# Second attention of a two-layer block: order of the rotary products, of the last stage's weight pieces, and of P times keys and projection

## What is computed

```python
def xattn(q, kv, seg_id, ...):                      # second layer, b=4, lq=256, lk=64, 16 heads
    q_c = q @ W_dq                                  # 256 -> 96
    q_rope = _rope((q_c @ W_qr).reshape(...))       # 64 rotary columns a head
    scores = (q_nope . k_nope + q_rope . k_rope) / sqrt(192)
    attn = softmax(where(in_window, scores, NEG))
    return (attn @ v).reshape(b, lq, H * HD) @ W_o
def _rope(x): x1, x2 = halves(x); return concat(x1*cos - x2*sin, x1*sin + x2*cos)
def ffn(x): return qlinear(silu(qlinear(x, gate)) * qlinear(x, up), down)    # 256 -> 704 -> 256
x = x + xattn(layernorm(x), ctx, seg_id); x = x + ffn(layernorm(x))
```

## Time and profile before

| | us |
|---|---|
| median of three runs (range) | 849.6 (848.35 to 850.79) |
| the profiled execution | 852.24 |
| its span, first to last instruction | 850.4 |
| TensorE busy | 790.1 (93%) |
| VectorE busy | 661.8 (78%) |
| ScalarE busy | 537.9 (63%) |
| GpSimd busy | 460.7 (54%) |

### The profile page before, as it was taken

The page is one execution under the profiler, slowest core; times in us unless marked ns, Lnnn a source line. Parts: engine busy times, 40 slices in busy tenths (PEclk is TensorE's granted clock), DMA queues, the critical chain, the costliest instruction groups (busy, mean ns, idle before and its releaser), DMA issues.

```text
span 850.4 us, 14334 instructions
## 1 busy us (share of the span) xinstructions
PE 790.1 (93%) x4848; PEld 676.2 (80%) x4848; DVE 661.8 (78%) x1584; ACT 537.9 (63%) x1236; POOL 460.7 (54%) x759
## 2 busy tenths in 40 slices
PE   3777999999999999999899999999999999798998
PEld 2566888888888888888788878898888877577787
DVE  7988888899888998879789794866654689966534
ACT  6888877788768886788674555433332278864332
POOL 3585869779686896858755576442210016970000
PEclk9779999999999999999999999999999999899999
DMA  7000120011200120000200324966421010100001
GB/s 239 14 1 1 38 75 1 2 39 42 72 1 1 38 79 34 2 2 2 67 25 13 126 63 102 233 172 243 131 64 49 1 44 13 50 14 0 1 1 50
DMA packets 28265, 45.59 MB, mean 54 GB/s; under 512 B 3937, under 2 KB 18081, under 8 KB 28065
## 3 DMA queue, kind: packets, MB, share of 16 engines
q1 hardware_dynamic: 26800, 41.31, 16.5%
q10 hardware_dynamic: 1392, 3.37, 1.1%
HBM read 43.49 MB, written 1.18 MB: 53 GB/s over the span
## 4 chain that ended last, share of the span: by engine, by line
PE 60%; DVE 23%; ACT 10%; issue 4%; DMA 2%; SPq 1%; ACTq 0%; POOL 0%; DVEq 0%
PE PS L770 16%; PE PS L840 7%; PE PS L725 6%; PE PS L630 5%; PE PS L699 4%; PE PS L661 4%; PE PS L951 3%; PE PS L671 2%; DVE cat L1541 2%; PE PS L652 2%; PE PS L682 2%; PE PS L709 2%; DVE st L1635 1%; DVE yb L1537 1%; DMA l_KM<-share 1%
## 5 line engine op out<-in xcount | busy, mean ns | idle before, releaser
L2222 POOL TENSOR_SCALAR raw<-raw,mvq,rsq 128x128 f32<-128x128 f32 x312 | 186.8, 612 | 7.2 <-DVE mvq L1682 5.7
L770 PE MATMUL PS<-xq,WH 128*128 128x512 f32 x472 | 148.4, 396 | 1.0 <-ACT l_x2T L995 1.0
L770 PEld LDWEIGHTS PS<-xq,WH 128*128 128x128 f32 x472 | 86.4, 190 | 18.1 <-issue 2.1
L770 PE MATMUL PS<-xq,WL 128*128 128x512 f32 x236 | 92.4, 391 | 0.0
L630 PE MATMUL PS<-WH,xq 128*128 128x256 f32 (+1 forms) x256 | 89.3, 367 | 2.6 <-issue 1.5
L630 PE MATMUL PS<-WL,xq 128*128 128x256 f32 (+1 forms) x256 | 84.6, 348 | 0.0
L1109 ACT ACTIVATE P<-PS,sm 128x256 f32<-128x256 f32 x128 | 60.6, 491 | 30.4 <-DVE sm L1710 30.3
L1635 DVE BATCH_NORM_STATS2 st<-raw 128x6 f32<-128x128 f32 x320 | 71.9, 277 | 0.9 <-ACT raw L1081 0.9
L840 PE MATMUL PS<-xq,m_hh 128*128 128x256 f32 x384 | 69.8, 282 | 2.8 <-ACT m_hh L995 1.4
L725 PE MATMUL PS<-PH,cat 128*128 128x256 f32 x256 | 66.0, 296 | 5.8 <-DVE cat L1541 5.5
L699 PE MATMUL PS<-PT,vr 128*128 128x256 f32 x256 | 66.3, 381 | 0.7 <-ACT PT L995 0.7
(11 more groups left out here) (305 smaller groups left out, 2193.8 us busy)
## 6 DMA issues: line engine op xcount, KB each, us to landing
wst<-in_wgu SPq DMA_DIRECT2D x24, 256.0 KB, 3.8
l_KM<-share SPq DMA_DIRECT2D x16, 384.0 KB, 4.2
wst<-in_wall SPq DMA_DIRECT2D x18, 256.0 KB, 3.1
l_KM<-share SPq DMA_DIRECT2D x16, 256.0 KB, 5.1
dst<-in_wdn SPq DMA_DIRECT2D x24, 128.0 KB, 3.2
wst<-in_wkvx SPq DMA_DIRECT2D x8, 256.0 KB, 3.4
l_KM<-share SPq DMA_DIRECT2D x16, 128.0 KB, 4.3
m_pre<-in_wo ACTq DMA_DIRECT2D x1, 2048.0 KB, 8.4
```

What stands on the lines that cost most here:

```text
L770: t = e.matmul(PS[:, b, :], W[wi][:, gu, k, :], a[:, k, cols], start=(n == 0), stop=(n == 5))
L2222: t = e.tensor_scalar(v, v, mvq[:, par, n, 0:1], rsq[:, par, n:n + 1], ALU.add, ALU.mult)
```

## The change

In `turn_q` the two products with the sine of a part come first, then the two products with the cosine; the sine products no longer signal, and the sums on GpSimd wait for the PSUM bank that the cosine product frees. All nine weight pieces stand behind the last sum on GpSimd. The loop over chunks has 11 steps in place of 12: `values` and `project` come one or two places sooner, and `turn_p`, `f_turn`, `f_front` stand elsewhere in a step, with matching places in the streams of ScalarE and VectorE.

```diff
-FPIECES = ((0,), (1, 2), (3, 4), (5,), (6, 7, 8))
@@ late_order
-    for n in range(12):
+    for n in range(11):
+        if n in (5, 7, 9):
+            do("turn_p", n - 2)
         if n < 8:
             do("scores", n)
-        if n % 2 == 0 and n > 3:
-            do("values", (n - 4) // 2)
-        if 1 < n < 10:
+        if n in (2, 3):
             do("turn_p", n - 2)
         for m in QUERIES.get(n, ()):
             do("queries", m // 2, m % 2)
-        if n % 2 and n > 4:
-            do("project", (n - 5) // 2)
-        if n % 2 and n > 6:
-            do("f_turn", (n - 7) // 2)
-        if n > 9:
-            do("f_front", *FFN[n - 10])
+        if n % 2 == 0 and n > 3:
+            do("project", (n - 4) // 2)
+        if n in (4, 6, 8):
+            do("turn_p", n - 2)
+        if n % 2 == 0 and n > 5:
+            do("f_turn", (n - 6) // 2)
+        if n > 8:
+            do("f_front", *FFN[n - 9])
+        if n % 2 and n > 2:
+            do("values", (n - 3) // 2)
@@ scalar
-            for n in range(12):
-                if n % 2 == 0 and n > 3:
-                    take_lv((n - 4) // 2)
-                if 1 < n < 10:
+            for n in range(11):
+                if 1 < n < 10 and n not in (4, 6, 8):
                     take_lp(n - 2)
                 for m in QUERIES.get(n, ()):
                     swap_q(m // 2, m % 2)
+                if n == 9:
+                    gate_f(0)
+                if n % 2 and n > 2:
+                    take_lv((n - 3) // 2)
                 if n < 8:
                     exps2(n)
-                if n == 11:
+                if n in (4, 6, 8):
+                    take_lp(n - 2)
+                if n == 10:
                     split_g(0)
-                if n % 2 and n > 6:
-                    split_f((n - 7) // 2)
-                if n > 9:
-                    gate_f(n - 10)
+                if n % 2 == 0 and n > 5:
+                    split_f((n - 6) // 2)
+                if n == 10:
+                    gate_f(1)
@@ vector, turn_q
                 for u in range(2 * part, 2 * part + 2):
+                    s = tqs[4 * bb + u].rearrange("p (a t) -> p a t", a=2)
+                    w.wait_ge(swapped.sem, swapped.at[bb, u])
+                    t = e.tensor_tensor(s, s, sin, ALU.mult)
+                t.then_inc(dv.sem, 1)
+                dv.up()
+                for u in range(2 * part, 2 * part + 2):
                     n = 4 * bb + u
-                    two = [v.rearrange("p (a t) -> p a t", a=2) for v in (tqc[n], tqs[n])]
-                    b = w.filled(("qr", bb, u))
-                    q = PS[:, b, :].rearrange("p (a t) -> p a t", a=2)
                     if n > 3:
                         w.wait_ge(added.sem, added.at[units_q[n - 2 if n > 5 else n - 4]])
-                    w.wait_ge(swapped.sem, swapped.at[bb, u])
-                    e.tensor_tensor(two[0], q, cos, ALU.mult).then_inc(free[b], 1)
-                    e.tensor_tensor(two[1], two[1], sin, ALU.mult).then_inc(turned_q.sem, 1)
+                    b = w.filled(("qr", bb, u))
+                    e.tensor_tensor(tqc[n].rearrange("p (a t) -> p a t", a=2), PS[:, b, :].rearrange("p (a t) -> p a t", a=2),
+                                    cos, ALU.mult).then_inc(free[b], 1)
@@ vector, the loop
-            for n in range(12):
+            for n in range(11):
...
-                if n in (6, 8, 10):
-                    add_l((n - 6) // 2)
-                if n == 11:
+                if n in (5, 7, 9):
+                    add_l((n - 5) // 2)
+                if n == 10:
                     split_g(0)
-                if n % 2 and n > 6:
-                    split_f((n - 7) // 2)
-                if n == 11:
+                if n % 2 == 0 and n > 5:
+                    split_f((n - 6) // 2)
+                if n == 10:
                     add_l(3)
-                if n > 9:
-                    gate_f(n - 10)
+                if n > 8:
+                    gate_f(n - 9)
@@ gpsimd
-                    w.wait_ge(turned_q.sem, turned_q.at[bb, u])
+                    w.emptied(("qr", bb, u))
...
-                for j in FPIECES[n]:
-                    load_f(j)
+            for j in range(9):
+                load_f(j)
```

More of the change, by code:

```diff
@@ L513, in program @@
         swapped = count("swapped", [(bb, u) for bb in range(4) for u in range(4)])
-        turned_q = count("turned_q", [(bb, u) for bb in range(4) for u in range(4)])
         gated_5 = count("gated_5", range(2))
```

## The result

The changed kernel takes 870.2 us (median of four runs, 864.54 to 872.31) against 849.93 before: ratio 1.023, 95% interval 1.0179 to 1.0281. The direction was forecast, the size was not: 861.6 was predicted, with a range of 849 to 868. The latter has a span of 867.7 us, 17.3 more than the 850.4 before. `f_front(2,0)`, behind which both kernels do the same work, starts at 820.12 us against 802.90: all of the difference, 17.2 us, lies ahead of it.

The account below looks back on a forecast made before the run. It took TensorE's gaps to stand behind VectorE, which GpSimd holds up. X at 776.7 plus 37.8 us put f_front(2,0) at 814.5 against 802.90: +11.6, with a slow project(3) +12, on 849.6 gives 861.6; range 849 to 868.

Parts of the forecast that it names:

- TensorE up to the first f_turn: TensorE from 701.3: 55.4 us of work plus 5.6 of short gaps, reaching f_turn(0) at 762.6, 3.9 us of work ahead.
- Laying out from X on: Both engines from turn_p(5) to the start of f_front(2,0): 37.8 us, so 814.5 against 802.90 before.
- X: Time when turn_p(5) may start on TensorE, after add_l(0), soft(6) and scale(5) on VectorE: 776.7 us.
- add_l(0) beside the pieces: First feed-forward normalisation on VectorE: fourteen small instructions each held by a GpSimd one, 15.8 us in place of 4.8, +11.
- The products of turn_q: VectorE, queries: sine products no longer held by GpSimd sums, with missing weight pieces sparing about 4 us over the stretch.
- The weight pieces' own time and the sums: GpSimd: sums end at about 745.5, then 28 us of pieces run to 773 at the earliest.
- Not held: Rival: GpSimd pieces hardly hold the normalisation; -2 us, 847.5; chance 0.09 for 846 to 850.
- gaps closed: Rival: TensorE's earlier project and values fill three gaps, nothing held; about -6, 843.5; chance 0.09 for 840 to 846.
- the rival that had both normalisations held: Late pieces make add_l(1) on VectorE pay as well as add_l(0): +17, 866.6; chance 0.06 for 866 to 870.

Follow-up runs that it names:

- Experiment 2: Changed kernel with project(0) moved behind turn_p(2), turn_p(3) and scores(5), nothing else: 859.7 us, ratio 1.0101.
- Experiment 3: Changed kernel with project's output and f_turn's transposes in bank 7 for batches 0 and 2, bank 6 for 1 and 3: 865.0 us, ratio 1.0183.
- Experiment 1: Changed kernel with the nine weight pieces between the sums on GpSimd again, order and sine products as changed: 864.8 us, ratio 1.0171.
- experiment 11: Kernel before with all weight pieces behind the sums and nothing else: 856.7 us, ratio 1.0082.
- experiment 4: Kernel before with sine products first and all weight pieces behind the sums, old TensorE order and 12 steps kept: 854.4 us, ratio 1.0058.
- experiment 5: Kernel before with the sine products first alone, pieces between the sums and order as before: 852.1 us, ratio 1.0035.
- the mended order: Changed kernel with project(0) behind scores(5), project's output banks by turns, and pieces 3 to 8 only after the first normalisation: 852.9 us, ratio 1.0045.

## Why the prediction was wrong

**TensorE up to the first f_turn: this step failed.** The prediction listed gaps of 5.6 us, "none of the length that slowed TensorE before", and had project(0) start as soon as the queries ended. It counted the queries' waits for their own banks, but not the bank of project. Bank 7 carried queries (3,3), whose cosine product stands behind scale(3) on VectorE; the prediction itself put that product at 743.5 (measured 742.1), and never asked what else wanted the bank. The wait that it put at nothing was 6.05 us, and project(0) ran 2.6 us slow behind it. TensorE stood at `f_turn(0)` at 770.5 and not at 762.6 (the list itself sums to 762.3). Experiment 2 shows what this wait costs: without it the kernel is 10.5 us faster.

**Laying out from X on: the same omission.** 37.8 us were given, 820.12 - 777.05 = 43.1 were measured, so this term was 5.3 us short. project(2) was given 1.3 us of copies and 6.9 of work; it waited 3.5 us for bank 7 and took 10.08, 5.4 us more, which is the difference. Experiment 3 took 5.2 us back by a bank number.

**add_l(0) beside the pieces: right in kind, mis-sized.** 15.8 us were predicted from 754.55 on, 10.0 us measured from 761.73 on. Two errors are in it. It began 7.2 us later, for the first omission. And the sum counted one GpSimd instruction for each of fourteen small ones; in the trace six of the twelve smallest pass unheld. Experiment 1 prices the hold at 5.4 us net, experiment 11 the moved pieces at 7.8 on the old order. X came out as 776.7 against 777.05 measured by luck: a missing 7.2 us against an excess of 5.8 in the chain and of 1.0 behind it, where scale(5) was to be held once more and the pieces were over.

**The products of turn_q: right over its stretch, no gain at the end.** About 4 us were given for the new form together with the missing pieces. In experiment 4, which has both, project(0) starts 41.5 us behind the first scores, before 45.4 (746.63 less 701.28): 3.8 us. Neither does it alone: 46.2 with the sine products first (experiment 5), 44.9 with the pieces away (experiment 11). Waits further on take the gain back: alone the new form is a loss of 0.35%.

**The weight pieces' own time and the sums** were right: the sums ended at 744.1 (745.5 predicted), the pieces at 773.0 (773).

**The rivals.** "Not held" and "gaps closed" are excluded by the trace. The time is just above the rival that had both normalisations held (866 to 870), for another reason: `add_l(1)` met no pieces and took 4.8 us. The forecast of a loss was right, but it was argued from a hold that lengthened the chain by 5.2 us and not by 11, while two bank waits that cost some 14 us by their rows (6.05 + 2.6, and 3.5 + 3.0 less 1.3 for copies) were missing. The losses taken out one at a time sum to 10.5 + 5.4 + 5.2 = 21.1 us by the medians, all together to 17.3; by the stage of the profiled executions it is 7.4 + 3.6 + 3.5 = 14.5 against 17.9. So the three account for most of the loss, but whether they overlap is not shown. What stays open is why the mended order is still 0.45% slower than before; its waits for copies fit the size, and so does the 0.35% of the sine products first, and no run took either away.

## What to carry to other kernels

When a producer is moved ahead in an order that also deals out PSUM banks, write down for each moved fill who held the bank last and where that release stands on its engine; here the release, not the data, cost most. A block of GpSimd work that is moved belongs beside VectorE work like soft, whose scalings out of PSUM (L2085) took 1.27 us for two beside L2353 and 1.28 without it, not beside a chain of small two-tensor instructions. And a wait taken away on TensorE pays only up to the next one: look at what the engine then meets, as soft(7) behind `add_l(0)` here.

## What the runs showed of the hardware

A small VectorE instruction that is held goes through with the end of GpSimd's instruction, and the one behind it passes unheld when GpSimd leaves a gap of 0.08 to 0.09 us: L1607 ended at 765.61, L1611 ran from 765.64 to 765.80, and L2349 of GpSimd, 0.09 us behind its predecessor's end, started at 765.69. Where GpSimd's instructions follow without such a gap (L2353 ends 765.02, L2345 starts 764.99) the next small one was held. In this chain all five such gaps between 763.6 and 769.7 let one through, and both places without a gap held. GpSimd leaves the gap where its next instruction waits for the one before; that this is the reason is argued from the kernel, no run changed it. So seven small ones went beside four GpSimd instructions (764.99 to 769.02), and the chain took 10.0 us in place of the 15.8 predicted. The hold goes both ways: L2349 of GpSimd, 1.27 us elsewhere, took 2.37 from 760.59 on, beside the product of scale(4) (L2101, 760.59 to 761.82). The Trainium skill, GPSIMD Engine Reference, section 1, names two-port modes besides two SBUF inputs; the hold of a small tensor_scalar instruction with one SBUF tensor, L1501 at 1.12 us against 0.17, fits that, but no row shows in which mode it ran.

After a wait of 3.5 to 6.5 us project took 8.8 to 10.2 us in five profiles of these kernels in place of 7.1, so such a wait cost another 0.4 to 0.9 of its own length behind itself. The granted clock of the changed kernel was 0.73 over project(0) and 0.70 over project(2), part of each at the lower level, and 1.00 over project(1). After 1.25 to 1.83 us of waiting project took 7.14 to 7.17 us, at a clock of 1.00 where it was read, but 8.83 at 0.80 once (the last one in experiment 3).
